# Attention cores of layers 2 to 4: scores built up over a chain of key tiles, maxima read in bank pairs, part of the softmax sum kept in PSUM

## The chip, the cores and the metric

One core of a Trainium2 chip runs the whole program. The metric is device time of one execution in microseconds. The kernel before took 2236.99 us in the median of three runs (2236.87 to 2241.3).

## What is computed

Four transformer layers of a gated cross-attention model over 16 batches of 56 tokens of width 256. Each layer adds an attention to a context of 1500 positions (64 wide), then a feed-forward part (64 experts with capacity, a ternary-weight layer, 16 experts, 8 experts). The attention of layers 2 to 4 is this, with H = 16 heads and R = 64:

```python
q_r = jnp.einsum('bshq,hqr->bhsr', q_big, W_qr)
k_r = jnp.einsum('bld,hdr->bhlr', kv_rope, W_kr)
scores = jnp.einsum('bhsr,bhlr->bhsl', q_r, k_r)
attn = jax.nn.softmax(scores, axis=-1)
ctx_c = jnp.einsum('bhsl,bld->bhsd', attn, kv_rope)
```

W_kr is folded into the queries, so that the keys of every head are the same 1500 x 64 matrix kv_rope, and so are the values.

## The kernel before

Five engines run programs of their own, held together by semaphores. `core_order` (used by all of them) writes out the order of one core, that is of the attention of one layer after the queries are made; an engine picks from it what it has to do. "Layer 2" is n = 1 in the code, and so on to n = 3.

A core treats the 16 batches one after another. The 1500 keys are NL = 12 tiles of LP = 125, and the 16 heads x 56 tokens are T = 896 columns in two halves of HT = 448, one for even and one for odd heads. Half 0 of the queries lies in partitions 0 to 63 and half 1 in 64 to 127, and the keys are there twice, so that two matmuls of 64 rows can run side by side. Keys and queries are split into a high and a low part (KH, KL, QH, QL).

**Scores half of a batch.** For each tile `head` (`pe_core`, line 1464) multiplies KH by QH and KL by QH, and `scores` KH by QL and a row of ones by M, which subtracts the maximum of each query. That is four products of two halves each, in two PSUM banks: 0, 1 and 2, 3 in turn. ScalarE takes the exponential of both banks into one of twelve tiles E (line 1915). Between the tiles PE computes the products of the next batch whose maxima are wanted, with the high parts alone: queries in seven columns of 128, of which three are even heads, three odd heads, and the fourth, the "ends", both halves together (QD, block-diagonal, 128 rows, line 1396). Each is taken against three chunks of 500 keys (CW): 21 products (18 on line 1392), each in one of banks 5, 6, 7, and VectorE reduces each by itself (line 2460), so a product waits for the reduction three places before it (`small`).

**Values half.** `values` multiplies the twelve E tiles by V into bank 4 (line 1474). Meanwhile VectorE gathers the maxima (`max_total`, nm), PE spreads them over partitions (`max_spread`, line 1444), VectorE makes M of that (line 2470). The sum over keys: GpSimd adds E tiles 0 to 7 into SA one by one as they come (line 2198), VectorE adds tiles 8 and 9 to one SB (line 2478, before the values) and 10 and 11 to another (behind values 8), and GpSimd adds both to SA. For the last batch SA and both SB go into the matmul instead. `total` (line 1490) sums SA over partitions one batch later, behind values 2 of the next batch; VectorE takes the reciprocal (RS, line 2482) and, behind values 8, divides the evicted values OB of the batch before by it (`div`, QR<-OB,RS, line 2487). ScalarE evicts bank 4 to OB (`evict`, line 1904) before the exponentials of the next batch, once `div` of the batch before it has read OB. The engines are in order, so on VectorE a batch goes: three end maxima and 18 side maxima, nm, SB, RS, M, SB, QR.

The keys are made in the stage of layer 1's experts (`context_order`): `crot` (GpSimd) and `cadd` (VectorE) turn the context by rotary embedding into V, `cturn` (PE) transposes V, ScalarE and VectorE split it into kt, and SP stores it to memory, from where each core loads KH and KL.

```python
        for k in range(NL):
            if sides and k % 4:
                t, c = sides.pop(0)
                order += [("max", b + 1, t, c), ("max", b + 1, t + 4, c)]
            order += [("head", b, k), ("scores", b, k)]
```

## Time and profile before

| | |
|---|---|
| median of three runs | 2236.99 us |
| profiled execution, first to last instruction | 2239.2 us |
| runs | 2241.3, 2236.99, 2236.87 us |
| busy: PE, VectorE, ScalarE, GpSimd | 2127.8, 1578.0, 1001.3, 1458.1 us |
| mean granted TensorE clock | 0.977 of full |
| instructions | 36249 |

The execution's own time is its span; what lies around it is not listed apart, and the span lies within the spread of the three runs. PE is TensorE, DVE VectorE, ACT ScalarE, POOL GpSimd; PEld are weight loads. Times in the rows below are microseconds from the span's start. The three cores run from about 432 to 823, from 1060 to 1451 and from 1730 to 2121.

### The profile page before, as it was taken

To read this page: it belongs to the slowest core of one execution; us is meant where nothing else is said; L and a number is where in the kernel's file an instruction comes from. 1 tells how busy PE (TensorE), PEld (TensorE's weight loads), DVE (VectorE), ACT (ScalarE), POOL (GpSimd) and SP (SyncE) were. 2 spreads that over 40 slices of the span, in tenths; PEclk is the share of its full clock that TensorE was granted. 3 is DMA by queue.
4 is the path that set the end of the run, shared out by engine and by line. 5 is a ranking of instruction groups with operands and counts; after the bars stand their busy time and mean duration, and the time that the engine had idled before them with its cause. 6 is when DMAs were issued, how large, how long until landed. Compare 5 with 4: busy or idle time off the path is not lost.

```text
span 2239.2 us, 36249 instructions
## 1 busy us (share of the span) xinstructions
PE 2127.8 (95%) x13972; PEld 1504.9 (67%) x13972; DVE 1578.0 (70%) x2546; ACT 1001.3 (45%) x1530; POOL 1458.1 (65%) x879
## 2 busy tenths in 40 slices
PE   7898999899999998898999999999997999999998
PEld 5686777656656665665665665588895656665588
DVE  6766863588888857666888888653334888888653
ACT  4452333445544545211554554444433554554443
POOL 0356763288888884463888888734441888888744
PEclk9899999999999999998999999999998999999999
DMA  3036875332232104002223222035523232222012
GB/s 94 19 103 197 258 246 142 78 79 56 56 82 57 42 29 133 24 1 60 56 69 70 56 58 67 16 89 149 152 65 74 56 77 63 56 66 60 19 53 79
DMA packets 65708, 179.65 MB, mean 80 GB/s; under 512 B 11280, under 2 KB 21280, under 8 KB 65154
## 3 DMA queue, kind: packets, MB, share of 16 engines
q1 hardware_dynamic: 65154, 177.01, 29.7%
q8 instruction: 112, 1.84, 0.3%
q10 hardware_dynamic: 384, 0.33, 0.1%
q14 instruction: 58, 0.48, 0.1%
HBM read 162.32 MB, written 14.98 MB: 79 GB/s over the span
## 4 chain that ended last, share of the span: by engine, by line
PE 81%; DVE 7%; issue 3%; POOL 3%; ACT 3%; DMA 1%; SPq 0%; POOLq 0%; DVEq 0%; ACTq 0%
PE psum L1464 22%; PE psum L926 19%; PE psum L1474 19%; PE psum L1392 6%; PE psum L1631 2%; PE psum L1396 2%; PE psum L1588 2%; PE psum L1490 2%; PE psum L940 1%; PE psum L1319 1%; PE psum L1197 1%; POOL CL L1937 1%; DMA bd<-in_blockdiag 1%; ACT E L1915 1%; DVE mx L2444 1%
## 5 line engine op out<-in xcount | busy, mean ns | idle before, releaser
L2198 POOL TENSOR_TENSOR SA<-SA,E 125x896 f32<-125x896 f32 x288 | 641.1, 2226 | 19.1
L2460 DVE TENSOR_REDUCE mx<-psum 128x1 f32<-128x500 f32 x945 | 566.6, 669 | 79.9 <-PE psum L1392 72.5
L1915 ACT ACTIVATE E<-psum 125x896 f32<-125x896 f32 x576 | 527.9, 920 | 164.4 <-PE psum L1464 163.4
L1474 PE MATMUL psum<-E,V 125*64 125x448 f32 x2304 | 459.4, 541 | 0.0
L1474 PEld LDWEIGHTS psum<-E,V 125*64 125x64 f32 x2304 | 159.9, 137 | 238.9 <-issue 213.1
L1464 PE MATMUL psum<-QH,KH 64*125 64x448 f32 x1152 | 298.3, 415 | 3.0 <-ACT E L1915 3.0
L1464 PE MATMUL psum<-QL,KH 64*125 64x448 f32 x1152 | 264.3, 363 | 0.0
L1464 PE MATMUL psum<-QH,KL 64*125 64x448 f32 x1152 | 264.2, 363 | 0.0
L1464 PE MATMUL psum<-M,ones 64*125 64x448 f32 x1152 | 263.8, 362 | 0.0
L1392 PE MATMUL psum<-KH,QH 64*128 64x500 f32 x864 | 234.2, 432 | 17.6 <-DVE mx L2444 17.3
L2198 POOL TENSOR_TENSOR SA<-SA,SB 125x896 f32<-125x896 f32 x90 | 199.7, 2219 | 53.0 <-DVE SB L2478 49.5
L2478 DVE TENSOR_TENSOR SB<-E,E 125x896 f32<-125x896 f32 x96 | 209.4, 2181 | 32.6 <-ACT E L1915 32.4
L1904 ACT ACTIVATE OB<-psum 128x448 f32<-128x448 f32 x45 | 24.6, 546 | 384.4 <-DVE QR L2487 362.4
L1464 PEld LDWEIGHTS psum<-QH,KH 64*125 64x125 f32 x1152 | 135.1, 182 | 72.0 <-ACT E L1915 52.0
L1392 PEld LDWEIGHTS psum<-KH,QH 64*128 64x128 f32 x864 | 137.0, 186 | 65.1 <-DVE mx L2460 20.9
L2198 POOL TENSOR_TENSOR SA<-E,E 125x896 f32<-125x896 f32 x48 | 101.8, 2120 | 107.3 <-ACT E L1915 103.1
L2248 POOL TENSOR_TENSOR HL<-HF,HH 128x448 fp32r<-128x448 f32 x70 | 81.1, 1161 | 132.1 <-ACT HH L2023 132.1
L2482 DVE RECIPROCAL RS<-psum 128x448 f32<-128x448 f32 x48 | 141.9, 2957 | 26.4 <-PE psum L1490 25.9
L1464 PEld LDWEIGHTS psum<-QL,KH 64*125 64x125 f32 x1152 | 153.4, 183 | 9.0
L1464 PEld LDWEIGHTS psum<-M,ones 64*125 64x125 f32 x1152 | 153.5, 183 | 8.5
L1464 PEld LDWEIGHTS psum<-QH,KL 64*125 64x125 f32 x1152 | 154.1, 184 | 0.6
L2698 DVE TENSOR_TENSOR HF<-R,psum 128x448 f32<-128x448 f32 x62 | 38.3, 620 | 129.5 <-PE psum L926 109.8
(303 smaller groups left out, 4069.8 us busy)
## 6 DMA issues: line engine op xcount, KB each, us to landing
KH<-kt_scratch SPq DMA_DIRECT2D x96, 375.0 KB, 5.1
KL<-kt_scratch SPq DMA_DIRECT2D x96, 375.0 KB, 6.8
EW<-in_f_w SPq DMA_DIRECT2D x64, 256.0 KB, 8.5
kt_scratch<-kt SPq DMA_DIRECT2D x16, 750.0 KB, 7.3
WS<-in_f_w SPq DMA_DIRECT2D x31, 384.0 KB, 5.1
GB<-gates_scratch SPq DMA_DIRECT2D x36, 224.0 KB, 3.8
slot_of_t<-slots_scratch SPq DMA_DIRECT2D x64, 112.0 KB, 4.4
WoT<-in_a_WoT SPq DMA_DIRECT2D x24, 256.0 KB, 3.7
```

Of the source, the lines that this page charges most:

```text
L926: i = e.matmul(o, a, b, start=start and n == 0, stop=stop and n == len(pairs) - 1, **kw)
L1392: return e.matmul(psum[:, bank, 0:CW], QH[b % 3][rows, q:q + P], KH[b % 3][rows, c * CW:(c + 1) * CW], start=True, stop=True)
L1396: return e.matmul(psum[:, bank, 0:CW], QD[b % 2][:, :], KH[b % 3][:, c * CW:(c + 1) * CW], start=True, stop=True)
L1464: i = e.matmul(psum[0:LP, pair + odd, 0:HT], keys[rows, which], queries[rows, odd * shift:odd * shift + HT], start=kind == "head" and x == ...
L1474: i = e.matmul(psum[c * DC:(c + 1) * DC, 4, 0:HT], V[0:LP, b, k * DC:(k + 1) * DC], E[g[n, b, k] % NE][0:LP, half[c]], start=k == 0, stop= ...
L1490: i = e.matmul(psum[c * DC:(c + 1) * DC, bank, 0:HT], ones[0:LP, 0:DC], x[0:LP, half[c]], start=x is terms[0], stop=x is terms[-1])
L1915: e.activation(E[m % NE][0:LP, :].rearrange("p (c q) -> p c q", c=2), psum[0:LP, pair:pair + 2, 0:HT], ACT.Exp).then_inc(exp_set.sem, 1)
L2198: e.tensor_tensor(SA[b % 2][0:LP, :], a[0:LP, :], x[0:LP, :], ALU.add).then_inc(sum_set.sem, 1)
L2248: e.tensor_tensor(m["HL"][u][:, :], m["HF"][u][:, :], m["HH"][u][:, :].bitcast(F32), ALU.subtract).then_inc(hl_set.sem, 1)
L2460: e.tensor_reduce(mx[:, b % 2, j * 3 + c:j * 3 + c + 1], psum[:, bank, 0:CW], AX.X, ALU.max).then_inc(small_free.sem, 1)
L2478: e.tensor_tensor(SB[list(PAIRED).index(k)][0:LP, :], e0, e1, ALU.add).then_inc(pair_set.sem, 1)
L2482: e.reciprocal(RS[:, :], psum[:, bank, 0:HT]).then_inc(small_free.sem, 1)
```

## The change

- The stored keys of tiles 4 to 11 are differences: tile t minus tile t - 4 (`cdelta`, GpSimd, one subtraction of 125 x 512 a batch, in the stage of layer 1's experts; `cturn` transposes them and waits for it). 
- Scores of tiles 4 to 11 are added to what the same two banks hold from tile t - 4. The order of the tiles is 0, 1, 4, 5, 8, 9, 2, 3, 6, 7, 10, 11, so that even places keep banks 0, 1 and odd places banks 2, 3. The product with M is only in tiles 0 to 3.
- Maxima: chunks of 500 keys are four tiles apart, so chunks 1 and 2 pile up on chunk 0 as well. Even and odd heads go to two neighbouring banks (6, 7 or 4, 5) and one reduction reads both. The ends are two 64-row halves in bank 5, one ahead of `head`, one behind it. Twelve steps in all; each waits for the reduction two steps before. Bank 4 being one of them, its first step waits for the eviction. In the first maxima of a core the ends take one to three products a chunk.
- `total` and `max_spread` use banks 0 and 1, so `head` of place 0 waits for M, and `head` of place 1 for the sum in banks 2, 3 of the batch before.
- Sum: ScalarE takes the exponential of the last place a second time, in place in banks 2, 3 (`again`). Behind `total` of the batch before, VectorE adds E of places 10 and 9 to these banks, in place, and with E of place 8 writes SB. GpSimd adds places 1 to 7 as before, and SB as the eighth.

Below is the diff's core. Left out are the declarations of flags and memory, the first maxima's order of indices, the sum of the last batch (SA and the one SB), and the waits of GpSimd and ScalarE that only change their flag's name.

```diff
-PAIRED = {9: (8, 9), 11: (10, 11)}
+TILES = (0, 1, 4, 5, 8, 9, 2, 3, 6, 7, 10, 11)
+CHAIN = 4
+OWN_SUM = 8
 FIRST = 10
-ADDED = (1, 2, 3, 4, 5, 6, 7, 9, 11)
+ADDED = (1, 2, 3, 4, 5, 6, 7, 11)
 LAST_ADDED = 7
+STEPS = [("max", 0, 0), ("max", 1, 0), ("max", 0, 1), ("max", 1, 1), ("max", 0, 2), ("max", 1, 2),
+         ("max", 2, 0), ("max_end", 0), ("max", 2, 1), ("max_end", 1), ("max", 2, 2), ("max_end", 2)]
+STEPS_AT = {0: (0,), 1: (1,), 2: (2,), 3: (3,), 4: (4,), 6: (5,), 7: (6,), 8: (7,), 9: (8,), 10: (9,), 11: (10, 11)}
...
+        delta = [("cdelta", b + 1)] if b + 1 < B else []
+        steps += [first + [("cturn", b, 0)], delta, last, [("cturn", b, 1)], []]
...
-        sides = [(t, c) for t in range(3) for c in range(3)] if b + 1 < B else []
         if b + 2 < B:
             order.append(("load_keys", b + 2))
         if b + 1 < B:
             order.append(("load_lows", b + 1))
-            order += [("max", b + 1, 3, c) for c in range(3)]
         for k in range(NL):
-            if sides and k % 4:
-                t, c = sides.pop(0)
-                order += [("max", b + 1, t, c), ("max", b + 1, t + 4, c)]
-            order += [("head", b, k), ("scores", b, k)]
+            steps = [STEPS[x] for x in STEPS_AT.get(k, ())] if b + 1 < B else []
+            order += [("max", b + 1, *t[1:]) for t in steps if t[0] == "max"]
+            order += [("low_end", b + 1, *t[1:]) for t in steps if t[0] == "max_end"]
+            order.append(("head", b, k))
+            order += [("max_end", b + 1, *t[1:]) for t in steps if t[0] == "max_end"]
+            order.append(("scores", b, k))
             if k == 4 and b + 1 < B:
                 order.append(("low", b + 1))
+        order.append(("again", b))
-        order.append(("add", b, 9))
         for k in range(NL):
             order.append(("values", b, k))
             if k == 1 and b + 2 < B:
                 order += [("high", b + 2), ("diag", b + 2)]
-            if k == 2 and b > 0:
-                order.append(("total", b - 1))
+            if k == 2:
+                order += [("total", b - 1)] if b > 0 else []
+                order.append(("add", b))
             if k == 7 and b + 1 < B:
                 order.append(("max_spread", b + 1))
             if k == 8:
-                order.append(("add", b, 11))
...
-    SB = [mem.take("SB", [P, T], F32) for _ in range(2)]
+    SB = mem.take("SB", [P, T], F32)
...
+    def small_bank(kind, b):
+
+        if kind == "total":
+            return 0 if b < B - 1 else 1
+        return 5 if b == 0 else 1
+
+    def max_banks(kind, *t):
+
+        return slice(5, 6) if kind == "max_end" else slice(4, 6) if t[0] == 1 else slice(6, 8)
...
-        return e.matmul(psum[:, bank, 0:CW], QH[b % 3][rows, q:q + P], KH[b % 3][rows, c * CW:(c + 1) * CW], start=True, stop=True)
-
-    def pe_ends(e, b, c, bank):
-
-        return e.matmul(psum[:, bank, 0:CW], QD[b % 2][:, :], KH[b % 3][:, c * CW:(c + 1) * CW], start=True, stop=True)
+        return e.matmul(psum[:, bank, 0:CW], QH[b % 3][rows, q:q + P], KH[b % 3][rows, c * CW:(c + 1) * CW], start=c == 0, stop=True,
+                        skip_group_check=True)
+
+    def pe_ends(e, b, c, bank, first):
+
+        return e.matmul(psum[:, bank, 0:CW], QD[b % 2][:, :], KH[b % 3][:, c * CW:(c + 1) * CW], start=first, stop=True,
+                        skip_group_check=True)
+
+    def pe_half_ends(e, b, c, odd):
+
+        rows = slice(odd * DC, (odd + 1) * DC)
+        return e.matmul(psum[:, 5, 0:CW], QD[b % 2][rows, :], KH[b % 3][rows, c * CW:(c + 1) * CW], start=(c, odd) == (0, 0), stop=True,
+                        skip_group_check=True)
+
+    def step_free(e, n, b, step):
+
+        x = STEPS.index(step)
+        if x >= 2:
+            kind, *t = STEPS[x - 2]
+            e.wait_ge(*small_free.at(n, kind, b, *t))
...
+                pair, c = t
+                step_free(e, n, b, (kind, pair, c))
+                if (pair, c) == (0, 0):
                     e.wait_ge(*kh_in.at(n, b))
                     e.wait_ge(*high_set.at(n, b))
-                    if made and b == 1:
+                    if b >= 2:
+                        e.wait_ge(*small_free.at(n, "max_end", b - 1, 2))
+                    elif made:
                         e.wait_ge(*q_set.at(*made[-1]))
-                if j == 3:
-                    if c == 0:
-                        e.wait_ge(*diag_set.at(n, b))
-                    i = pe_ends(e, b, c, bank)
-                else:
...
+            elif kind == "low_end":
+                c, = t
+                step_free(e, n, b, ("max_end", c))
+                if c == 0:
+                    e.wait_ge(*diag_set.at(n, b))
+                pe_half_ends(e, b, c, 0).then_inc(low_end_made.sem, 1)
+                lead = 1
+            elif kind == "max_end":
+                c, = t
+                e.wait_ge(*low_end_made.at(n, b, c))
+                pe_half_ends(e, b, c, 1).then_inc(small_made.sem, 1)
+                lead = 0
...
+                bank = small_bank(kind, b)
+                if b > 0:
+                    e.wait_ge(*exp_set.at(n, b - 1, NL - 2))
                 e.wait_ge(*nm_set.at(n, b))
...
-                pair, cols = 2 * (m % 2), slice(k * LP, (k + 1) * LP)
+                tile = TILES[k]
+                pair, cols = 2 * (m % 2), slice(tile * LP, (tile + 1) * LP)
                 if kind == "head":
                     if k == 0:
                         e.wait_ge(*kl_in.at(n, b))
+                        e.wait_ge(*small_free.at(n, "max_spread", b))
+                    if k == 1 and b > 0:
+                        e.wait_ge(*own_sum_set.at(n, b - 1))
                     if m >= 2:
                         e.wait_ge(*exp_set.at(*ks[m - 2]))
                     parts = [(KH[b % 3], cols, QH[b % 3], 0), (KL[b % 2], cols, QH[b % 3], 0)]
                 else:
                     if k == 0:
                         e.wait_ge(*low_set.at(n, b))
-                        e.wait_ge(*small_free.at(n, "max_spread", b))
-                    parts = [(KH[b % 3], cols, QL[b % 2], 0), (ones_r, slice(0, LP), M[b % 2], DC)]
+                    parts = [(KH[b % 3], cols, QL[b % 2], 0)] + ([(ones_r, slice(0, LP), M[b % 2], DC)] if tile < CHAIN else [])
                 for x, (keys, which, queries, shift) in enumerate(parts):
                     for odd in (lead, 1 - lead):
                         rows = slice(odd * DC, (odd + 1) * DC)
                         i = e.matmul(psum[0:LP, pair + odd, 0:HT], keys[rows, which], queries[rows, odd * shift:odd * shift + HT],
-                                     start=kind == "head" and x == 0, stop=kind == "scores" and x == 1)
+                                     start=kind == "head" and x == 0 and tile < CHAIN, stop=kind == "scores" and x == len(parts) - 1,
+                                     skip_group_check=True)
                 if kind == "scores":
...
                 if k == 0 and b > 0:
                     e.wait_ge(*evicted.at(n, b - 1))
+                if k == 0 and b + 1 < B:
+                    e.wait_ge(*small_free.at(n, "max", b + 1, 1, 2))
                 for c in range(2):
-                    i = e.matmul(psum[c * DC:(c + 1) * DC, 4, 0:HT], V[0:LP, b, k * DC:(k + 1) * DC],
...
+            elif kind == "again":
+                i = e.activation(psum[0:LP, 2:4, 0:HT], psum[0:LP, 2:4, 0:HT], ACT.Exp)
+                i.then_inc(again_set.sem, 1)
...
-                if k in PAIRED:
-                    x = SB[list(PAIRED).index(k)]
-                    e.wait_ge(*pair_set.at(n, b, k))
+                if k >= OWN_SUM:
+                    x = SB
+                    e.wait_ge(*own_sum_set.at(n, b))
                 else:
...
+            elif kind == "cdelta":
+                b, = t
+                e.wait_ge(*v_set.at(b))
+                if b >= 2:
+                    e.wait_ge(*v_turned.at(b - 2, 1))
+                e.tensor_tensor(steps_of[b % 2][0:LP, :], V[0:LP, b, CHAIN * DC:NL * DC], V[0:LP, b, 0:(NL - CHAIN) * DC],
+                                ALU.subtract).then_inc(steps_set.sem, 1)
...
+                by_side = mx[:, b % 2, :].rearrange("p (j c) -> p j c", c=3)
+                o = by_side[:, t[0]:t[0] + 5:4, t[1]] if kind == "max" else by_side[:, 3:4, t[0]]
+                e.tensor_reduce(o, psum[:, max_banks(kind, *t), 0:CW], AX.X, ALU.max).then_inc(small_free.sem, 1)
...
-                k = t[0]
-                e.wait_ge(*exp_set.at(n, b, k))
+                e.wait_ge(*again_set.at(n, b))
                 if b >= 1:
-                    e.wait_ge(*sum_set.at(n, b - 1, k))
-                e0, e1 = (E[g[n, b, x] % NE][0:LP, :] for x in PAIRED[k])
-                e.tensor_tensor(SB[list(PAIRED).index(k)][0:LP, :], e0, e1, ALU.add).then_inc(pair_set.sem, 1)
+                    e.wait_ge(*sum_set.at(n, b - 1, NL - 1))
+                acc = psum[0:LP, 2:4, 0:HT]
+                for k in (10, 9, 8):
+                    x = E[g[n, b, k] % NE][0:LP, :].rearrange("p (c q) -> p c q", c=2)
+                    if k > OWN_SUM:
+                        e.tensor_tensor(acc, acc, x, ALU.add).then_inc(*dve_own.up())
+                        e.wait_ge(*dve_own.now())
+                    else:
+                        e.tensor_tensor(SB[0:LP, :].rearrange("p (c q) -> p c q", c=2), acc, x, ALU.add).then_inc(own_sum_set.sem, 1)
```

## Rows read from the trace of the kernel before

**Rows 1.** The page: busy time by engine, and the chain by line.

```profile
PE 2127.8 (95%) x13972; PEld 1504.9 (67%) x13972; DVE 1578.0 (70%) x2546; ACT 1001.3 (45%) x1530; POOL 1458.1 (65%) x879
...
PE psum L1464 22%; PE psum L926 19%; PE psum L1474 19%; PE psum L1392 6%; PE psum L1631 2%; PE psum L1396 2%; PE psum L1588 2%; PE psum L1490 2%; PE psum L940 1%; PE psum L1319 1%; PE psum L1197 1%; POOL CL L1937 1%; DMA bd<-in_blockdiag 1%; ACT E L1915 1%; DVE mx L2444 1%
```

**Rows 2.** Windows, one batch: busy us, clock, DMA share, GB/s.

```profile
525.00:549.36 24.36, 24.36 (x179) 15.21 (x175) 21.28 (x28) 12.67 (x16) 21.01 (x11) 1.00 0.28 65
```

**Rows 3.** Timeline of PE: start us, us, instructions; out<-in, count.

```profile
576.80 0.95 PE L1396 MATMUL psum<-KH,QD 128*128 128x500 f32 x3
...
583.32 0.47 PE L1464 MATMUL psum<-QH,KH 64*125 64x448 f32 x2
...
584.04 0.36 PE L1464 MATMUL psum<-M,ones 64*125 64x448 f32 x2
...
591.04 2.48 PE L1474 MATMUL psum<-E,V 125*64 125x448 f32 x12
```

**Rows 4.** Timeline of ScalarE, same batch; idle before and releaser in brackets.

```profile
577.38 0.55 ACT L1904 ACTIVATE OB<-psum 128x448 f32<-128x448 f32 x1 [8.54 <-DVE QR L2487]
578.80 0.92 ACT L1915 ACTIVATE E<-psum 125x896 f32<-125x896 f32 x1 [0.87 <-PE psum L1464]
...
582.34 1.85 ACT L1915 ACTIVATE E<-psum 125x896 f32<-125x896 f32 x2 [0.25 <-PE psum L1464]
...
584.44 0.92 ACT L1915 ACTIVATE E<-psum 125x896 f32<-125x896 f32 x1 [0.25 <-PE psum L1464]
```

**Rows 5.** Timeline of VectorE, same batch and its neighbour.

```profile
569.93 2.96 DVE L2482 RECIPROCAL RS<-psum 128x448 f32<-128x448 f32 x1 [0.41 <-PE psum L1490]
...
573.91 0.69 DVE L2470 TENSOR_TENSOR M<-psum,bd 128x512 fp32r<-128x512 f32 x1 [1.02 <-PE psum L1444]
574.52 2.23 DVE L2478 TENSOR_TENSOR SB<-E,E 125x896 f32<-125x896 f32 x1
576.67 0.61 DVE L2487 TENSOR_TENSOR QR<-OB,RS 128x448 f32<-128x448 f32 x1
577.34 5.36 DVE L2460 TENSOR_REDUCE mx<-psum 128x1 f32<-128x500 f32 x9
583.48 3.61 DVE L2460 TENSOR_REDUCE mx<-psum 128x1 f32<-128x500 f32 x6 [0.79 <-PE psum L1392]
...
591.69 2.48 DVE L2478 TENSOR_TENSOR SB<-E,E 125x896 f32<-125x896 f32 x1
...
594.31 2.96 DVE L2482 RECIPROCAL RS<-psum 128x448 f32<-128x448 f32 x1
```

**Rows 6.** Timeline of GpSimd, same batch.

```profile
573.71 2.09 POOL L2198 TENSOR_TENSOR SA<-SA,SB 125x896 f32<-125x896 f32 x1
...
576.90 2.37 POOL L2198 TENSOR_TENSOR SA<-SA,SB 125x896 f32<-125x896 f32 x1 [1.09 <-DVE SB L2478]
```

**Rows 7.** Timelines, layer 2: first score; VectorE and GpSimd in the last batch.

```profile
432.25 0.47 PE L1464 MATMUL psum<-QH,KH 64*125 64x448 f32 x2
...
815.15 3.21 POOL L1937 TENSOR_TENSOR CL<-QR,CH 128x1024 fp32r<-128x1024 f32 x1
...
816.07 2.77 DVE L2487 TENSOR_TENSOR QR<-OB,RS 128x448 f32<-128x448 f32 x1
...
822.00 0.62 DVE L2487 TENSOR_TENSOR QR<-psum,RS 128x448 f32<-128x448 f32 x1
```

**Rows 8.** Lines 2444, 2698, 2198: min, median, max ns.

```profile
L2444 DVE TENSOR_REDUCE mx<-psum x30: 1187/1190/1722, 414.2 to 1724.8; 128x2 f32<-128x1000 f32 x27, 128x3 f32<-128x1500 f32 x3
...
L2698 DVE TENSOR_TENSOR HF<-R,psum x62: 606/621/622, 1483.2 to 2226.4; 128x448 f32<-128x448 f32 x62
...
L2198 POOL TENSOR_TENSOR SA<-SA,SB x90: 2082/2111/2381, 452.6 to 2095.1; 125x896 f32<-125x896 f32 x90
```

**Rows 9.** Layer 1's experts, 200 to 360 us: line group of GpSimd, PE's waits.

```profile
L2269 POOL TENSOR_TENSOR ctx_rot<-V,sin_k 125x384 f32<-125x384 f32 x12 | 13.8, 1149 | 27.1 <-DVE V L2760 27.1
...
PE psum L1631 <- DVE YDL L2743: 4.9, 6, 1.9
```

More of the change, by code:

```diff
@@ L152, in context_order @@
 def context_order():
-    steps = [[("cload", b) for b in range(4)], [("crot", 0)], [("cadd", 0), ("cload", 4)], [("crot", 1)], [("cadd", 1)]]
+    steps = [[("cload", b) for b in range(4)], [("crot", 0)], [("cadd", 0), ("cload", 4)], [("crot", 1), ("cdelta", 0)], [("cadd", 1)]]
     for b in range(B):
@@ L159, in context_order @@
         last = [("cadd", b + 2)] if b + 2 < B else []
-        steps += [first + [("cturn", b, 0)], [], last, [("cturn", b, 1)], []]
+        delta = [("cdelta", b + 1)] if b + 1 < B else []
+        steps += [first + [("cturn", b, 0)], delta, last, [("cturn", b, 1)], []]
     return steps + [[("cstore", B - 1)]]
@@ L672, in build @@
     m["GT"] = mem.take("slots_turned", [E0, T], BF16)
+    at(v_end)
+    steps_of = [mem.take("key_steps", [P, (NL - CHAIN) * DC], F32) for _ in range(2)]
+    assert mem.at <= mh_end - 8 * 512
     SS = nc.dram_tensor("slots_scratch", (E0, T), BF16, kind="Internal").ap()
@@ L767, in build @@
     out0_low, out0_high = flag("out0_low", halves), flag("out0_high", halves)
-    small_uses = [(n, *t) for n, t in cores if t[0] in ("first", "max", "max_spread", "total")]
+    small_uses = [(n, *t) for n, t in cores if t[0] in ("first", "max", "max_end", "max_spread", "total")]
     small_made, small_free = flag("small_made", small_uses), flag("small_free", small_uses)
@@ L918, in upper @@
         return upper_bank[f, use]
-    small_ring = {n: [u for u in small_uses if u[0] == n and u[1] != "first"] for n in layers}
-    small_at = {u: m for n in layers for m, u in enumerate(small_ring[n])}
+    def small_bank(kind, b):
[4 more added lines that the diff above has]
+        return slice(5, 6) if kind == "max_end" else slice(4, 6) if t[0] == 1 else slice(6, 8)
     def product(e, o, pairs, start=True, stop=True, **kw):
@@ L1418, in pe_core @@
                     for c in range(3):
[L1419 removed]
+                        for upto in range(c + 1):
+                            i = pe_ends(e, b, upto, banks[c], upto == 0)
                 else:
                     for odd in range(2):
[L1422 removed]
+                        i = pe_side(e, b, p % 3 + 4 * odd, p // 3, banks[odd])
                 i.then_inc(small_made.sem, 1)
             elif kind == "max":
[L1425 removed]
@@ L1439, in pe_core @@
-                i.then_inc(small_made.sem, 1)
+                if (pair, c) == (1, 0):
+                    e.wait_ge(*(evicted.at(n, b - 2) if b >= 2 else small_free.at(n, "max_spread", 0)))
+                banks = range(8)[max_banks(kind, pair)]
+                for odd in range(2):
+                    i = pe_side(e, b, pair + 4 * odd, c, banks[odd])
+                i.then_inc(small_made.sem, 1)
+                lead = 0
[10 more added lines that the diff above has]
+                pe_half_ends(e, b, c, 1).then_inc(small_made.sem, 1)
+                lead = 0
@@ L1477, in pe_core @@
             elif kind == "total":
-                bank = small(e, n, kind, b)
+                bank = small_bank(kind, b)
+                e.wait_ge(*exp_set.at(n, min(b + 1, B - 1), NL - 2))
                 if (n, b) == (1, 0):
@@ L1918, in added @@
     def added(n, b, k):
-        for last, pair in PAIRED.items():
-            if k in pair:
-                return pair_set.at(n, b, last)
-        return sum_set.at(n, b, max(k, 1))
+        return own_sum_set.at(n, b) if k >= OWN_SUM else sum_set.at(n, b, max(k, 1))
     def act_part(e, n, i):
@@ L2481, in dve_core @@
                     e.wait_ge(*o_divided.at(n, b - 1))
-                e.reciprocal(RS[:, :], psum[:, bank, 0:HT]).then_inc(small_free.sem, 1)
+                e.reciprocal(RS[:, :], psum[:, small_bank(kind, b), 0:HT]).then_inc(small_free.sem, 1)
             elif kind == "div":
```

46 lines of the change are left out of this document (17 added, 29 removed).

## Prediction

> **What bounds the kernel now.** I read the page first. PE is busy for 95% of the span, and three of the four largest shares of the chain that ended last (lines 1464, 1474 and 1392: 22%, 19% and 6%) lie in the attention cores of layers 2 to 4 [rows 1]. Then the windows: in one steady stretch of 24.36 us PE is busy throughout, at a granted clock of 1.00, VectorE 21.28, GpSimd 21.01, ScalarE 12.67 [rows 2]. That stretch is one batch, and it repeats: the reciprocal starts at 569.93 and at 594.31, 24.38 us apart [rows 5], and the fifteen batches of each layer that follow one another keep this beat (24.37 between most). So there is little slack anywhere, and a busy PE proves nothing. I take the batch apart by engine.
>
> PE has two halves. The scores half goes from the three end products at 576.80 to 591.04, 14.2 us; the values half, with the sum of the batch before and the spread in it, takes the other 10.1 us [rows 3]. In the scores half a tile issues four products, each a pair of 64-row halves side by side: the first takes 0.3 us after its wait, the others 0.21 (583.32 to 584.04 is three pairs), a pair of 500-column side products 0.22. ScalarE starts an exponential 0.4 us after the last pair has started (584.04, 584.44), takes 0.92, and the next tile in the same banks starts 0.06 after that (582.34 + 0.92 = 583.26, and 583.32) [rows 3, 4]. That loop is 1.12 + 0.92 + 0.06 = 2.1 us for two tiles, and with the side products in the same stream a tile takes 1.1 to 1.17. VectorE idles twice for 0.8 us in the scores half (583.48) [rows 5], so today it is nearly, but not quite, what sets this half.
>
> VectorE in the values half: a sum (SB), the reciprocal of 2.96 us, the spread (M), a second sum, the division (QR), and then at once nine maxima in 5.36 us, 0.60 each [rows 5]. The second sum starts at 574.52, and takes 2.23 us for 896 elements, though a spread of 512 elements takes 0.69. The reason stands in GpSimd's rows: its add runs from 573.71 to 575.80, and the VectorE sum ends 0.95 after that end [rows 5, 6]. It has waited for the whole add. The last batch of layer 2 shows the same for the division: it starts at 816.07 inside a GpSimd subtraction that ends at 818.36, and takes 2.77 us, ending 0.48 after it [rows 7], where 0.61 is normal at 576.67, when GpSimd is idle until 576.90 [rows 5, 6]. Operations with one input in PSUM never do this: HF<-R,psum is 606 to 622 ns in all 62 [rows 8], and M at 573.91 took its 0.69 with GpSimd's add running.
>
> **What the change removes.** Eight of twelve tiles lose the product with M: one pair each, 8 x 0.205 = 1.64 us of PE a batch, 1.64 x 48 = 79 us if PE alone counted. The 21 single maxima become nine over two banks and three single ones. A maximum over 1000 elements is 1.19 us [rows 8], back to back 1.12 (0.07 overlaps, as in 5.36 for nine); 9 x 1.12 + 3 x 0.60 = 11.9 against 21 x 0.60 = 12.5. The three full end products become three pairs of halves, which slot between head and scores: equal, 0.22 each. GpSimd loses one of nine adds. ScalarE gains one exponential (0.92 at most) behind tile 11, where it is idle for 8.5 us [rows 4]: nothing.
>
> **What it adds on VectorE.** Two SB sums go (2.23 and 2.48 us, half of it waiting) [rows 5]; three adds come, with one input in PSUM, the first two in place. Nearest rows: 0.62 for 448 elements and 0.69 for 512 with a PSUM input, so 0.155 + 896 / 960 = 1.09 each; two waits on its own result between them, 0.1 each. 3 x 1.09 + 0.2 = 3.5. No row writes PSUM from VectorE. Low bound 0.95 (the part of an SB sum that runs free), high bound 2.2 (an SB sum as it is). I take 1.09, from the PSUM-input rows, since input kind and count are the same.
>
> **What moves, and where it collides.** The three adds stand behind the reciprocal, not around it, and the last releases GpSimd's add of tile-slot 11. GpSimd starts slot 1 when the second exponential is done, 9.3 us before this point's zero by the times below, and needs seven adds of 2.11 [rows 8] and the one for QL, some 16 us: it has ended slot 7 by 7.0, waits there and goes 0.15 later, as it does now behind SB (576.75, 576.90) [rows 5, 6]. VectorE goes on with the spread (0.62, PSUM input, free), and then the division meets an add that has 1.6 us to run. Today the division is ahead of that add; afterwards it is behind it. With the values half starting at 0:
> - reciprocal from 3.3 (594.31 - 591.04) to 6.2 [rows 3, 5]; adds to 9.7; GpSimd 9.85 to 11.95; division ends 0.48 later, 12.4. Today it ends at 10.6.
> - The division frees OB: eviction 0.10 later and 0.55 long [rows 4], to 13.1. Today 0.87 us of slack follow before the first exponential (577.93, 578.80). This slack is used up: the scores of tile 0 are done at 11.7, their exponential waits to 13.1, and PE waits too, since bank pair 4, 5 of the second maximum holds the values until the eviction. Late next is therefore the whole scores half.
> - Maxima steps 0 to 9 on VectorE from 12.4: eight at 1.12, two at 0.60, 10.2 us, with four gaps of 0.2 to 0.4 where the step before on the same banks or the eviction releases PE late, 1.2 us in all: 23.85. Only then may PE start the last half end (a step waits for the step two before it), then head and scores of slot 11: 0.06 + 0.2 + 0.41 + 0.1 + 0.2 = 1.0 us. Values start at 24.9.
> So a batch takes 24.9 where it took 24.37: +0.54. PE waits about 2 us of it; the 1.6 us saved are all in there.
>
> I laid the old order out by the same durations as a test of the method: 24.33 us a batch, and 390 us from first score to last division, where the trace has 24.37 and 390.4 (432.25 to 822.62) [rows 7].
>
> **The sum.** Thirteen steady batches a layer x 0.54 = +7.0. The first scores half has no division or eviction before it and is 1.4 us shorter (eight pairs less), the first period 0.9 shorter: -2.3. The last batch: its scores start late by the same collision, less the eight pairs, +0.6; and the last sum comes at 9.7 instead of some 1.2 us earlier, so reciprocal and division end 1.2 later: +1.8. +6.5 a layer, +19.5 for three. In the stage of layer 1's experts GpSimd gets 16 subtractions of 512 elements: 384 take 1.15 and 896 take 2.11, so 1.39 each, 22 us. It is waiting there for V for 27.1 us and PE waits only 4.9 us, for YDL [rows 9]: cover enough, unless the new operations hold up VectorE's two-input ones in their turn. I take +2, bounds 0 and +12. Sum +22. The profiled run's span was 2239.2, so 2261; the median of the runs is 2237.0, 2 us below, so **2259 us**.
>
> The Trainium skill says why the division waits ("SBUF — State Buffer", "SBUF: two separate sides"): VectorE with two SBUF inputs and a GpSimd operation that reads SBUF exclude each other for a whole instruction, whichever starts first. By that rule, the trace agrees (0.48 and 0.95 us behind the GpSimd end), it is the start that counts. A split of bandwidth would give the division about 1.2 us instead of 2.1 and a batch near 24.
>
> **Rivals.** (a) *The division gets through*: it starts before the add, or the add is late. Then it ends at 10.9, the evict slack stays, and my layout gives 23.33 a batch, -15 us a layer: 2237 - 44 + 2 = 2195, faster. For: the batch now has just this order at 576.67. Against: 0.15 us from sum to add, 0.62 from sum to division. It decides where the division ends before 11.9 (24.37 a batch); chance 0.25. (b) *PE is the limit, its 79 us come back*: 2160. Against: ScalarE's loop and the chain of steps two apart; 0.05. (c) *In-place adds in PSUM cost 2.0 or more*: three times 0.9 more, period 27.7, +49 a layer by the same layout: 2237 + 147 + 2 = 2386. For: no row has the form. 0.05. (d) *The two effects cancel*: adds of 0.95 give 24.5 a batch and +1.4 a layer, 2243; 0.1.
>
> **The numbers.** Forecast 0.55. The range holds (a) and the forecast with adds up to 1.2 us (25.3 a batch, +37) and +12 in the first stage: 2192 to 2290; outside lie (b), (c) and a remainder. A measurement tells about 0.2% (4.5 us) from no change. Slower: forecast and (c), 0.6; faster: (a), (b), 0.3; within: 0.1.
>
> **What would show it.** Right: SB's last add 9.5 to 10 us after the values start; the division 2.0 to 2.2 us long and ending 0.5 us behind GpSimd's last add of the batch; OB eviction with the first exponential right behind it; PE idle about 1.5 us, released by that eviction; a period near 24.9; adds of 1.09. Wrong: divisions of 0.61; a period under 24.2; PE waiting for exponentials alone in the scores half; adds near 2 us; the first expert stage longer than before by over 12 us.

## Result and the profile after

| | before | after |
|---|---|---|
| median of four runs each | 2236.93 us (2234.36 to 2241.3) | 2272.9 us (2272.86 to 2275.63) |
| ratio, 95% interval | | 1.016 (1.0144 to 1.0177) |
| profiled execution, first to last instruction | 2239.2 us | 2273.8 us |
| first score to last division, the three cores | 390.4, 391.9, 390.4 us | 399.6, 399.6, 398.7 us |
| first score of layer 2 at | 432.25 us | 442.50 us |

Slower by 36 us, where 22 were forecast. Of the 34.6 us between the profiled spans, 10.25 are there when the first core starts, and the three cores add 25.2. (The profile of experiment 4 fell on a disturbed execution, so that kernel ran a second time, as e10.) The page of the kernel after, as [rows 1]:

```profile
PE 2067.7 (91%) x13336; PEld 1418.4 (62%) x13336; DVE 1577.2 (69%) x2189; ACT 1024.5 (45%) x1578; POOL 1344.7 (59%) x850
...
PE 59%; DVE 18%; issue 11%; ACT 5%; POOL 3%; DMA 2%; SPq 0%; DVEq 0%; POOLq 0%; ACTq 0%
```

PE has lost 60 us of work, VectorE is busy for as long as before, GpSimd for 113 us less. No engine works for the whole span. Now one batch, as [rows 2] (length, PE, PE's loads, VectorE, ScalarE, GpSimd, granted clock, DMA share, GB/s):

```profile
575.00:600.02 25.02, 23.07 (x161) 13.25 (x160) 21.31 (x21) 13.14 (x19) 18.11 (x11) 1.00 0.27 62
```

The batch has grown from 24.36 to 25.02 us, and PE, which was busy for all of it, now stands still for 2 us of it. The timelines show where; the values half of this batch starts at 602.97. VectorE, as [rows 5] (start, us, operation; in brackets the idle time before and who ended it):

```profile
606.24 2.96 DVE L2544 RECIPROCAL RS<-psum 128x448 f32<-128x448 f32 x1 [2.42 <-PE psum L1540]
609.12 2.21 DVE L2537 TENSOR_TENSOR psum<-psum,E 125x896 f32<-125x896 f32 x2
611.36 1.09 DVE L2540 TENSOR_TENSOR SB<-psum,E 125x896 f32<-125x896 f32 x1
612.37 0.68 DVE L2527 TENSOR_TENSOR M<-psum,bd 128x512 fp32r<-128x512 f32 x1
612.97 2.21 DVE L2549 TENSOR_TENSOR QR<-OB,RS 128x448 f32<-128x448 f32 x1
615.10 5.82 DVE L2517 TENSOR_REDUCE mx<-psum 128x2 f32<-128x1000 f32 x5
```

GpSimd, as [rows 6]:

```profile
603.00 6.42 POOL L2249 TENSOR_TENSOR SA<-SA,E 125x896 f32<-125x896 f32 x3
612.60 2.10 POOL L2249 TENSOR_TENSOR SA<-SA,SB 125x896 f32<-125x896 f32 x1 [3.17 <-DVE SB L2540]
```

ScalarE, as [rows 4], and PE one batch earlier, as [rows 3]:

```profile
615.27 0.54 ACT L1958 ACTIVATE OB<-psum 128x448 f32<-128x448 f32 x1 [9.31 <-DVE QR L2549]
615.71 0.91 ACT L1969 ACTIVATE E<-psum 125x896 f32<-125x896 f32 x1
```

```profile
588.09 0.49 PE L1403 MATMUL psum<-KH,QH 64*128 64x500 f32 x2
...
590.85 0.50 PE L1403 MATMUL psum<-KH,QH 64*128 64x500 f32 x2 [1.45 <-ACT OB L1958]
```

Read them as one chain. SB is done at 612.45; GpSimd, idle for 3.17 us, adds it from 612.60 to 614.70; the division starts at 612.97 inside that add and ends at 615.18, 0.48 behind it; the eviction of OB starts 0.09 later; the first exponential starts right behind the eviction; and PE's second maximum, whose banks include the one that is evicted, waits 1.45 us. It does so in every steady batch (39 times), and 42 of the 45 divisions take the long form. PE's waits and all 45 divisions and 96 in-place adds (min, median, max ns):

```profile
PE psum L1403 <- ACT OB L1958: 56.5, 39, 1.5
...
L2549 DVE TENSOR_TENSOR QR<-OB,RS x45: 613/2214/2223, 487.9 to 2151.4; 128x448 f32<-128x448 f32 x45
...
L2537 DVE TENSOR_TENSOR psum<-psum,E x96: 1072/1099/1100, 457.2 to 2149.2; 125x896 f32<-125x896 f32 x96
```

### The profile page after: what moved, and what is told of

Its sections match the earlier page's. It is cut to its first block, busy times and chain, and to the rows that moved or that the text cites. A ratio compares the mean times of both kernels' runs of the same rounds, so it can differ in the third digit from the quotient of the medians.

```text
span 2273.8 us, 34565 instructions
## 1 busy us (share of the span) xinstructions
PE 2067.7 (91%) x13336; PEld 1418.4 (62%) x13336; DVE 1577.2 (69%) x2189; ACT 1024.5 (45%) x1578; POOL 1344.7 (59%) x850
## 4 chain that ended last, share of the span: by engine, by line
PE 59%; DVE 18%; issue 11%; ACT 5%; POOL 3%; DMA 2%; SPq 0%; DVEq 0%; POOLq 0%; ACTq 0%
PE psum L944 19%; PE psum L1509 15%; PE psum L1523 6%; DVE psum L2537 4%; DVE QR L2549 4%; PE psum L1403 4%; PE psum L1414 3%; PE psum L1681 3%; ACT E L1969 2%; PE psum L1540 2%; PE psum L1638 2%; DVE mx L2517 1%; DVE M L2527 1%; ACT OB L1958 1%; PE psum L958 1%
## 5 line engine op out<-in xcount | busy, mean ns | idle before, releaser
L2249 POOL TENSOR_TENSOR SA<-SA,E 125x896 f32<-125x896 f32 x288 | 605.1, 2101 | 19.1
L2517 DVE TENSOR_REDUCE mx<-psum 128x2 f32<-128x1000 f32 (+1 forms) x540 | 551.5, 1064 | 66.3 <-PE psum L1414 33.6
L1509 PE MATMUL psum<-QH,KH 64*125 64x448 f32 x1152 | 254.7, 408 | 14.9 <-ACT E L1969 14.2
L1509 PE MATMUL psum<-QH,KL 64*125 64x448 f32 x1152 | 222.7, 364 | 0.0
L1403 PEld LDWEIGHTS psum<-KH,QH 64*128 64x128 f32 x864 | 92.3, 186 | 136.6 <-ACT OB L1958 71.3
L2249 POOL TENSOR_TENSOR SA<-SA,SB 125x896 f32<-125x896 f32 x45 | 94.6, 2103 | 132.1 <-DVE SB L2540 131.9
L1414 PE MATMUL psum<-KH,QD 64*128 64x500 f32 x270 | 114.0, 422 | 15.4 <-DVE mx L2517 15.4
L2309 POOL TENSOR_SCALAR S<-slot_of_t,slots 128x896 fp32r<-128x896 bf16 x32 | 98.1, 3069 | 42.0 <-DMA slot_of_t<-slots_scratch 31.3
L1509 PEld LDWEIGHTS psum<-QH,KL 64*125 64x125 f32 x1152 | 117.2, 184 | 7.2
L2537 DVE TENSOR_TENSOR psum<-psum,E 125x896 f32<-125x896 f32 x96 | 104.4, 1087 | 4.7 <-ACT psum L1952 3.0
```

The source lines that it names most:

```text
L1403: return e.matmul(psum[:, bank, 0:CW], QH[b % 3][rows, q:q + P], KH[b % 3][rows, c * CW:(c + 1) * CW], start=c == 0, stop=True, skip_group ...
L1414: return e.matmul(psum[:, 5, 0:CW], QD[b % 2][rows, :], KH[b % 3][rows, c * CW:(c + 1) * CW], start=(c, odd) == (0, 0), stop=True, skip_gr ...
L1509: i = e.matmul(psum[0:LP, pair + odd, 0:HT], keys[rows, which], queries[rows, odd * shift:odd * shift + HT], start=kind == "head" and x == ...
L2249: e.tensor_tensor(SA[b % 2][0:LP, :], a[0:LP, :], x[0:LP, :], ALU.add).then_inc(sum_set.sem, 1)
L2309: e.tensor_scalar(m["S"][q % 3][:, :], m["PB"][q % 3][:, :], m["slots"][:, CAP0:CAP0 + 1], None, ALU.is_equal).then_inc(s_set.sem, 1)
L2517: e.tensor_reduce(o, psum[:, max_banks(kind, *t), 0:CW], AX.X, ALU.max).then_inc(small_free.sem, 1)
```

## Experiments

**Theory:** the last GpSimd add of a batch, let go 0.5 us ahead of the division, makes the division wait, and this alone turns the change from a gain into a loss. **Rivals:** PE's work sets the batch; the division is late because the adds stand ahead of it, and waiting costs nothing more; the sum in PSUM is dear; the new GpSimd subtractions are. Each run lists its ratio to the kernel before with a 95% interval; "us" beside a ratio is (ratio - 1) x 2237, so that kernels of different chips compare. The batch is the interval between two reciprocals in the middle of layer 2.

| kernel | median us | ratio (95%) | us | batch |
|---|---|---|---|---|
| after | 2272.9 | 1.016 (1.0144, 1.0177) | +36 | 25.02 |
| 1: GpSimd's last add behind the division | 2209.89 | 0.9872 (0.9855, 0.9888) | -29 | 23.41 |
| 2: no key differences | 2267.68 | 1.0133 (1.0114, 1.0153) | +30 | 25.0 |
| 3: one product fewer in eight tiles | 2252.28 | 1.0058 (1.0041, 1.0074) | +13 | 24.45 |
| 4: division ahead of the adds | 2234.85 | 0.9986 (0.9972, 0.9999) | -3 | 23.86 |
| 5: 1, and the sum of the batch before earlier | 2197.57 | 0.9812 (0.979, 0.9833) | -42 | 23.31 |
| 6: 1, with the sum in SBUF | 2227.24 | 0.9945 (0.9913, 0.9976) | -12 | 23.62 |
| 7: 5, first subtraction earlier | 2195.46 | 0.9802 (0.9779, 0.9826) | -44 | 23.31 |
| 8: before, without M in eight tiles | 2229.72 | 0.9954 (0.9929, 0.9979) | -10 | 24.16 |
| 9: 7, first maximum in the values half | 2215.16 | 0.9897 (0.9876, 0.9917) | -23 | 23.64 |

**1. The add waits for the division.** GpSimd has one wait more; no work is taken away.

```diff
                 if k >= OWN_SUM:
                     x = SB
                     e.wait_ge(*own_sum_set.at(n, b))
+                    if b > 0:
+                        e.wait_ge(*o_divided.at(n, b - 1))
```

> GpSimd's last add of a batch waits for the division as well as for SB; nothing else differs from the changed kernel (2272.9 us, 25.02 us a batch). Theory A, the exclusive pair of the division and that add is what the batch pays: the division takes 0.61 instead of 2.21 us, the eviction starts 1.5 us earlier, a batch takes 23.3 to 23.6, and the kernel 65 us less than the changed one, 2200 to 2215. Rival B, PE and ScalarE set the scores half and the division is only along for the ride: the division is short, but the batch stays within 0.2 us of 25.0 and the kernel above 2262. Rival C, GpSimd's add is late next: slot 1 of the next batch waits for it and the time saved comes back as waits for SA; 2240 to 2260.

VectorE and GpSimd in the same batch of layer 2, and all divisions:

```profile
605.79 1.09 DVE L2542 TENSOR_TENSOR SB<-psum,E 125x896 f32<-125x896 f32 x1
606.80 0.68 DVE L2529 TENSOR_TENSOR M<-psum,bd 128x512 fp32r<-128x512 f32 x1
607.40 0.61 DVE L2551 TENSOR_TENSOR QR<-OB,RS 128x448 f32<-128x448 f32 x1
...
608.18 2.12 POOL L2251 TENSOR_TENSOR SA<-SA,SB 125x896 f32<-125x896 f32 x1 [4.26 <-DVE QR L2551]
...
L2551 DVE TENSOR_TENSOR QR<-OB,RS x45: 612/614/616, 490.4 to 2088.6; 128x448 f32<-128x448 f32 x45
```

Every division takes 0.61 us now, PE's wait for the eviction is gone from its list, and the batch is 1.6 us shorter: the same length as the division lost. The kernel is 64 us faster than after (63 by the medians), and 1.3% faster than before. GpSimd starts its add 1.3 us behind SB's end (606.88, 608.18), where it was 0.15 in after, and nothing waits for it. That is the theory's main claim, shown by a wait that only delays an engine.

**2. Key differences left out.** The keys of tiles 4 to 11 are whole ones, so the scores there are others. The first `cdelta`, in the list of the stage's first steps, is gone too.

```diff
-        delta = [("cdelta", b + 1)] if b + 1 < B else []
+        delta = []
...
-                e.wait_ge(*steps_set.at(b))
+                e.wait_ge(*v_set.at(b))
...
-                    src = V[0:LP, b, x * DC:(x + 2) * DC] if x < CHAIN else steps_of[b % 2][0:LP, (x - CHAIN) * DC:(x - CHAIN + 2) * DC]
+                    src = V[0:LP, b, x * DC:(x + 2) * DC]
```

> The changed kernel without the subtractions that make key differences (GpSimd, 16 times 1.29 us): the transposes take V as it is, so the scores of tiles 4 to 11 are computed from whole keys and the output is another. The cores run the same instructions. Theory A: layer 1's expert stage gets its 10 us back (first score of layer 2 at 432 instead of 442.5), 2262 to 2264, and the wait of 6.8 us of PE for key_steps is gone. Rival B: the 10 us come from PE's clock and from transfers, not from the subtractions: less than 4 us change.

It gave 5 us by the medians, 6 by the ratios, where 9 to 11 were expected, and the intervals of the two kernels overlap. PE's wait of 6.8 us for `key_steps` is gone from its list, with 3.4 us for V in its place, but the stage of layer 1's experts stayed long. The windows from 159 to 200 us, of before, after and this kernel in turn (columns as above):

```profile
159.00:200.00 41.00, 32.76 (x186) 26.66 (x186) 28.51 (x40) 7.92 (x16) 17.53 (x13) 0.92 0.51 135
```

```profile
159.00:200.00 41.00, 31.11 (x169) 25.35 (x170) 27.49 (x36) 5.07 (x10) 18.85 (x13) 0.83 0.47 122
```

```profile
159.00:200.00 41.00, 32.25 (x177) 25.98 (x175) 26.52 (x36) 6.28 (x13) 16.81 (x11) 0.83 0.50 132
```

The granted clock is the lower one of after, 0.83 against 0.92 (between 182 and 198 us it is 0.57 against 0.79, a mean of stretches at 1.2 and 2.4 GHz), though the subtractions are gone. The first score comes at 440.68, against 442.50 in after and 432.25 in before. But kernels whose program up to there is the same as after's have it at 444.93 (1), 440.11 (3), 441.97 (5) and 442.18 (6), and 8, with before's program there, at 434.31. One profile cannot tell 2 us in this stage. What the profiles show is 6 to 13 us between the two families. The subtractions do hold up the keys: the last store of kt is issued at 335.7 us in after, and at 327.2 here, 325.5 in before, 327.2 in 8. But the last product with YDH, further on in the experts, comes at 380.9 in after and still at 379.8 here, against 370.6 in before and 375.1 in 8. So in these profiles most of the longer stage is there without the subtractions, and what makes it stays open; their share, about 5 us by the times, isn't clear of the noise.

**3. PE gets less to do.** The product of KL with QH is left out in tiles 4 to 11.

```diff
-                    parts = [(KH[b % 3], cols, QH[b % 3], 0), (KL[b % 2], cols, QH[b % 3], 0)]
+                    parts = [(KH[b % 3], cols, QH[b % 3], 0)] + ([(KL[b % 2], cols, QH[b % 3], 0)] if tile < CHAIN else [])
```

> The changed kernel without the product of the low keys with the high queries in the eight tiles that add to their chain: one pair of matmuls less in each, 1.64 us of PE a batch, and the low part of these keys is missing from the scores. Theory A, VectorE's chain sets the batch and PE lies on it only between the last reduction it waits for and the next values: 0.2 to 0.8 us a batch less, 10 to 37 us in all, 2236 to 2263. Rival B, PE sets the batch: 1.64 us a batch, 75 us, below 2205. Rival C, PE is nowhere on it: within 5 us of 2273.

This takes as much from PE as the change itself did (8 x 0.205 us a batch, 79 us in all), and gives 23. PE's wait for the eviction stays as it was, and the division is long as often as in after (42 of 45):

```profile
PE psum L1403 <- ACT OB L1958: 56.6, 39, 1.5
...
608.87 8.12 DVE L2517 TENSOR_REDUCE mx<-psum 128x2 f32<-128x1000 f32 x7
```

With fewer products between them VectorE's maxima follow one another without the gaps of after, where five were in a row. The batch is 0.57 shorter of 1.64: about a third of PE's work came back in each batch, through those gaps as I read the rows, and the rest did not.

**4. The division ahead of the adds.** The time and ratio are of the first run of it, the profile of e10 (one execution, 2234.12 us).

```diff
-                order += [("total", b - 1)] if b > 0 else []
+                order += [("total", b - 1), ("div", b - 1)] if b > 0 else []
                 order.append(("add", b))
...
-                order += [("div", b - 1)] if b > 0 else []
```

> VectorE divides directly behind the reciprocal, ahead of the three adds, instead of behind the spread. The division then meets GpSimd's add of place 7 for up to 1 us instead of the last add for 1.6 us, and the eviction is free 5 us earlier. Theory A: the division takes 0.6 to 1.6 us, a batch 24.0 to 24.2, 2235 to 2245. Rival B, only the order of VectorE counts, not the lock: the sum of VectorE's work is the same, so the batch stays at 25.0 less what the eviction alone brings (under 0.3): above 2258.

> The kernel with the division directly behind the reciprocal once more, for a profile at the full clock, since the first one was taken on a disturbed run. Theory A as before: a batch of 24.0 to 24.3 us, the division waiting up to 1.6 us for GpSimd's add of place 7, the eviction ready before PE needs it, and no wait of PE for OB (56.5 us in the changed kernel). Rival B: a batch above 24.7.

VectorE, then GpSimd:

```profile
601.50 2.96 DVE L2543 RECIPROCAL RS<-psum 128x448 f32<-128x448 f32 x1 [2.42 <-PE psum L1539]
604.56 0.62 DVE L2548 TENSOR_TENSOR QR<-OB,RS 128x448 f32<-128x448 f32 x1
605.11 2.22 DVE L2536 TENSOR_TENSOR psum<-psum,E 125x896 f32<-125x896 f32 x2
...
608.97 1.19 DVE L2516 TENSOR_REDUCE mx<-psum 128x2 f32<-128x1000 f32 x1
...
598.27 6.43 POOL L2248 TENSOR_TENSOR SA<-SA,E 125x896 f32<-125x896 f32 x3
```

GpSimd's three adds end at 604.70, so the division, from 604.56, meets at most their end (0.62 to 0.92 us). The batch is 23.86, 1.2 shorter than after, with the same work, and somewhat under both expectations. It stays 0.45 above experiment 1, where the division starts as late as in after but is short. In the rows M is what became later: it starts 6.87 us behind the reciprocal's start here (608.37 - 601.50) and 6.13 in experiment 1 (606.80 - 600.67), and the first `head` waits for M. So an early division is not what matters, only one that doesn't meet GpSimd.

**5. The sum of the batch before two places earlier**, on top of experiment 1. VectorE idles 2.42 us before the reciprocal in after and in 1; does it matter?

```diff
-            if k == 2:
+            if k == 0:
                 order += [("total", b - 1)] if b > 0 else []
                 order.append(("add", b))
```

> As the kernel in which GpSimd's last add waits for the division (2209.9 us, 23.44 us a batch), and the total of the batch before stands behind values 0 instead of values 2, so that VectorE's idle time of 2.42 us ahead of the reciprocal shrinks to about 0.9. Theory A: VectorE then waits 0.8 us for the first maximum of the next batch instead; the chain of steps from there is the limit, and only 0.2 to 0.4 us a batch come back: 2192 to 2202. Rival B, VectorE's work is the limit everywhere: the whole 1.5 us come back, 2145. Rival C, the idle time was free: 2210 within 4.

```profile
595.73 2.96 DVE L2546 RECIPROCAL RS<-psum 128x448 f32<-128x448 f32 x1 [0.92 <-PE psum L1540]
```

The idle time fell by 1.5 us and the batch by 0.10, less than the 0.2 expected at least, and 4 us over the three cores. The kernel gained 12 by the medians. In its profile the first score came 3 us earlier, which is within what experiment 2 shows between equal programs, and the core of layer 2 lost 2.7 us, from 376.45 to 373.73, where thirteen batches make 1.2. The rest is the 1.5 us itself, once a core. From the first score to the first reciprocal it is 38.70 us in 1 (444.93, 483.63) and 37.21 here (441.97, 479.18), and at the core's end the time is not lost again. There the sum of the batch before, its adds, the last sum and the last division follow one another on VectorE with nothing else to do, and the two last reciprocals stay 8.12 and 8.11 us apart. The first of the two in experiment 1:

```profile
809.58 2.96 DVE L2546 RECIPROCAL RS<-psum 128x448 f32<-128x448 f32 x1 [14.32 <-PE psum L1540]
```

So the 2.42 us that look like the largest gap on VectorE were almost free in a steady batch, and counted in full in a core's last one: 1.5 us in each of three cores, beside the 4 us.

**6. The same sum in SBUF,** on top of 1. The second exponential is gone and the three adds read and write SBUF.

```diff
-                e.wait_ge(*again_set.at(n, b))
+                e.wait_ge(*exp_set.at(n, b, NL - 1))
...
-                acc = psum[0:LP, 2:4, 0:HT]
                 for k in (10, 9, 8):
-                    x = E[g[n, b, k] % NE][0:LP, :].rearrange("p (c q) -> p c q", c=2)
+                    x = E[g[n, b, k] % NE][0:LP, :]
+                    acc = E[g[n, b, NL - 1] % NE][0:LP, :] if k == 10 else SB[0:LP, :]
```

> As the kernel in which GpSimd's last add waits for the division (2209.9 us), but tiles 10, 9 and 8 are added to tile 11's exponential in SBUF, in SB, and the second exponential into PSUM is left out. Theory A: only the first of the three adds meets a GpSimd add (place 7) and waits up to 0.8 us, then GpSimd has nothing to do; 0.4 to 0.9 us a batch more, 2226 to 2250. Rival B: two inputs in SBUF are as quick as PSUM here, the lock does not matter for the adds: 2210 within 4. Rival C: every add waits, 2 us each, 3 us a batch: above 2330.

```profile
602.05 1.30 DVE L2535 TENSOR_TENSOR SB<-E,E 125x896 f32<-125x896 f32 x1
603.38 2.22 DVE L2535 TENSOR_TENSOR SB<-SB,E 125x896 f32<-125x896 f32 x2
...
595.97 6.44 POOL L2248 TENSOR_TENSOR SA<-SA,E 125x896 f32<-125x896 f32 x3
```

It is 17 us slower than 1: 0.21 a batch (8 us), where 0.4 at least was expected, and 3.7 at the end of each core, where two of the adds take 4.24 us beside a GpSimd subtraction (from 814.41, and 813.38 to 816.57). In the batch only the first add met GpSimd, whose run ends at 602.41, and paid 0.2 for it; the two behind it take 1.11 each, as from PSUM. In experiment 5 the adds in PSUM start at 598.61, beside GpSimd's run of adds from 594.02 to 600.46, and take 2.21 us for two all the same. PSUM saves meetings, not time per element.

**7. The first subtraction ahead of the second batch's rotation,** on top of 5.

```diff
-[("crot", 1), ("cdelta", 0)]
+[("cdelta", 0), ("crot", 1)]
```

> As the kernel with the early total, and in layer 1's expert stage the first key differences are made ahead of the second batch's rotation on GpSimd instead of behind it. Theory A: the first transposes come 1.9 us earlier and the wait of 6.8 us of PE is 4.9; 1 to 4 us less than the kernel with the early total. Rival B: PE then waits for YDL instead, no difference within 2 us.

PE's waits in 5, then in 7:

```profile
PE psum L1681 <- DVE YDL L2807: 10.3, 7, 3.1
...
PE psum L1706 <- POOL key_steps L2329: 6.6, 1, 6.6
```

```profile
PE psum L1681 <- DVE YDL L2807: 12.1, 7, 5.3
...
PE psum L1706 <- POOL key_steps L2329: 4.5, 1, 4.5
```

The wait for the differences lost 2.1 us and another gained 1.8. The intervals of 5 and 7 overlap, and 9, whose program is the same up to there, has its first score at 443.91, later than 5: nothing shown. At 2195.46 us it is the fastest measured, 2.0% below before.

**8. The kernel before without the product with M** in the eight tiles where the change drops it; the scores there lack their maximum.

```diff
-                    parts = [(KH[b % 3], cols, QL[b % 2], 0), (ones_r, slice(0, LP), M[b % 2], DC)]
+                    parts = [(KH[b % 3], cols, QL[b % 2], 0)] + ([(ones_r, slice(0, LP), M[b % 2], DC)] if k in (0, 1, 6, 7) else [])
```

> The kernel before, without the product of ones and M in places 2 to 5 and 8 to 11 of each batch, so these scores keep their maximum and their exponentials and the output are others; PE has 1.64 us less to do a batch, and nothing else changes. Theory A: ScalarE's loop and the single maxima hold the scores half, so only 0.1 to 0.3 us a batch come back, 2222 to 2234. Rival B, PE is the limit of the kernel before: 79 us less, below 2175.

```profile
570.00:594.20 24.20, 23.91 (x159) 13.58 (x157) 21.11 (x29) 12.45 (x16) 20.75 (x10) 1.00 0.29 67
```

PE lost its 1.64 us a batch, and the batch 0.2 of them: 7 us by the medians, 10 by the ratios, out of 79. But this run leaves more than PE changed. All 45 divisions in before, then here (in all and mean of one):

```profile
L2487 DVE TENSOR_TENSOR QR<-OB,RS 128x448 f32<-128x448 f32 x45 | 34.0, 756 | 0.0
```

```profile
L2487 DVE TENSOR_TENSOR QR<-OB,RS 128x448 f32<-128x448 f32 x45 | 83.6, 1859 | 0.0
...
599.48 2.51 DVE L2487 TENSOR_TENSOR QR<-OB,RS 128x448 f32<-128x448 f32 x1
```

With less on PE, VectorE and GpSimd meet otherwise: outside a core's last batch 26 of 42 divisions are long, and none in before, and the divisions and the SB sums together cost VectorE 56 us more, 1.2 a batch. The same collision as in the changed kernel eats into what PE gave, so the 0.2 does not tell how much of PE's time would have come back without it. Experiment 3, with 42 long divisions on either side, is the fairer one. What this run does show is that the busy time of PE is no proof that PE is the bound: after losing 1.64 us of products it is still shown busy for 23.91 of 24.20 us.

**9. The first maximum's product behind values 9,** on top of 7, so that VectorE has work right after the division.

```diff
+            if k == 9 and b + 2 < B:
+                order.append(("max", b + 2, 0, 0))
```

> As the kernel with GpSimd's add behind the division, the early total and the earlier key differences (2195.5 us, 23.31 us a batch, of which VectorE waits 1.57 us for the first maximum of a batch). The products of that first maximum now stand behind values 9 of the batch before, while VectorE is idle. Theory A, the chain of twelve steps from that maximum is the limit: VectorE starts it 1.3 us earlier and 0.5 to 1.3 us a batch come back, 2135 to 2172. Rival B, the scores half is by now held by PE and ScalarE, and the move costs PE two more changes between whole and half arrays: 0 to 0.4 us a batch more, 2195 to 2213.

VectorE and then PE:

```profile
607.02 1.20 DVE L2521 TENSOR_REDUCE mx<-psum 128x2 f32<-128x1000 f32 x1
609.92 4.52 DVE L2521 TENSOR_REDUCE mx<-psum 128x2 f32<-128x1000 f32 x4 [1.70 <-PE psum L1405]
...
606.49 0.49 PE L1405 MATMUL psum<-KH,QH 64*128 64x500 f32 x2
606.91 1.72 PE L1525 MATMUL psum<-E,V 125*64 125x448 f32 x8
608.56 0.47 PE L1511 MATMUL psum<-QH,KH 64*125 64x448 f32 x2
608.87 0.37 PE L1511 MATMUL psum<-QH,KL 64*125 64x448 f32 x2
```

The maximum runs early and VectorE then waits 1.7 us for the next: the batch is 0.33 longer, the kernel 20 us slower than 7, 2 us above rival B's range. The pair of 64-row products between 125-row ones holds PE for 0.42 us (606.49 to 606.91) where in after's scores half it holds it for 0.22 (592.00 and 592.22 in its timeline). If PE's order sets the batch at this place, that is 0.20 of the 0.33; where the rest arises isn't resolved. The Trainium skill ("TensorEngine Tiling (Array Packing)", "Key Properties") says that a change of tiling mode, not just of tile, drains TensorE. It gives no price; this trace agrees with it, at 0.20 us for a pair of 64-row products put between products of 125 rows.

## Why the prediction was right, and where its size was off

- **The division meets the add: right, and the decisive step.** Forecast from the start of the values half: SB ends 9.7, GpSimd 9.85 to 11.95, division ends 12.4, eviction to 13.1. Measured: 9.48, 9.63 to 11.73, 12.21, 12.84. The long division took 2.21 us, of which 0.61 is its own time in experiment 1. The rule of the Trainium skill cited in the prediction ("SBUF — State Buffer", "SBUF: two separate sides"), that the operation that starts first holds the other off whole, agrees here: a shared rate would not have ended the division 0.48 behind the add.
- **Adds of 1.09 in PSUM: right.** 1072 to 1100 ns in 96. Rival (c) falls, and with it its 2386.
- **Maxima: right.** Reductions of 1000 took 1.12 to 1.20 and step 9 ended at 23.75, forecast 23.85.
- **The last piece was mis-sized.** From step 9's end to the values I counted 1.0 us; it was 1.27 (601.7 to 602.97). The batch is therefore 25.02 and not 24.9: +0.64 instead of +0.54, which makes 8.2 a layer where 7.0 was forecast.
- **The ends of a core.** From the first score to the first reciprocal the change is -1.5, -2.3 and -1.6 us in layers 2, 3 and 4, forecast -2.3; behind the last steady batch it is +2.6, +1.7 and +1.7, forecast +1.8. So the start gave less than I took in two cores, and the end was about right. Together +25.2, forecast +19.5.
- **The experts' stage was the term furthest off.** I took +2, by the argument that GpSimd's wait for V covers 22 us of subtractions; the profile gave +10.25, inside the bound of 12. A subtraction took 1.29 us in the median, less than my 1.39, so their length was not the error. They stand between V and `cturn`, and PE waits 6.8 us for them once; cover on GpSimd over the stage says nothing on that one path. They do delay the keys, by 8 us at the last store, but without them (experiment 2) the first score comes only 1.8 us earlier in the profile and the kernel is 5 us faster, within overlapping intervals. So in the profiles most of this term stays without them, and no run shows what it is.
- **PE's 79 us: right that they don't come back.** Leaving out an equal amount gives 23 of 79 in experiment 3; the 7 to 10 of experiment 8 are too low a measure, as said there. Even the fastest kernel here, 7, stands at 2195, far above rival (b)'s 2160.
- **Rival (a), the division gets through,** was given 23.33 a batch and 2195. The kernel of experiment 1, which makes it true by a wait, has 23.41 and 2209.89; the layout was good to a tenth of a microsecond, and the gap in the total is the experts' stage again.

The sum forecast against measured, in the profiles: experts +2 and +10.25, cores +19.5 and +25.2, remainder 0 and -0.9 us.

## What to carry to other kernels

When an edit moves a VectorE operation that reads SBUF twice, look at which GpSimd operation the instructions just ahead of it release, and compare the two distances: here 0.15 us to the add and 0.5 to the division cost 1.6 us in each of 39 batches and turned a gain of 1.3% into a loss of 1.6%, and one wait that holds the idle engine back repaired it. A PE that is busy for a whole period is not thereby its bound: leave a product out and time it, before counting its time as gain, and look in that run's rows whether a new collision has swallowed the gain. A gap on an engine, be it 2.4 us in every batch, may be almost free in the steady beat and count in full in the last batch, where nothing else runs; follow the wait that PE ends up in.

## What the hardware showed that I had not expected

- A VectorE add in place in PSUM, 125 x 896, took 1.07 to 1.10 us, the same as the one that writes SBUF (1.09), and an exponential in place in PSUM 0.91 beside 0.92 to SBUF (medians of the kernel after).
- Two VectorE adds reading SBUF twice took 1.11 us each while GpSimd was idle (experiment 6), so a second SBUF input cost nothing by itself.
- One pair of 64-row products between 125-row ones held PE 0.20 us longer than between 64-row ones (experiment 9).
- Two programs whose instructions agree up to the first score reached it up to 4.8 us apart (440.11 and 444.93), both at a granted clock of 0.57 between 182 and 198 us; in 5, with 0.68 there, it came between them (441.97).
